# Global attention: maximum products in couples over four banks, score half steps over three

## What is computed

```python
h = NUM_HEADS                                   # 16 heads of 64
q = _split_heads(x @ Wq + bq, h)
k = _split_heads(x @ Wk + bk, h)
v = _split_heads(x @ Wv + bv, h)
pattern = jnp.einsum('bhid,bhjd->bhij', k, q) * scale
prob = jax.nn.softmax(pattern, axis=-2)         # over i, the k side
out = jnp.einsum('bhis,bhid->bhsd', prob, v)
concat = out.transpose(0, 2, 1, 3).reshape(b, s, h * dv)
return concat @ Wo + bo
```

## Time and profile before

| what | value |
|---|---|
| median of three runs | 5289.54 us (5285.4 to 5291.37) |
| profiled execution | 5297.28 us, span 5295.5 us |
| PE busy (share of the span) | 4716.1 us (89%) |
| DVE, ACT, POOL busy | 3549.8 (67%), 2216.3 (42%), 2746.9 us (52%) |
| mean granted clock of PE | 0.938 of 2.4 GHz |

### The profile page before, as it was taken

The page is one execution under the profiler, slowest core; times in us unless marked ns, Lnnn a source line. Parts: engine busy times, 40 slices in busy tenths (PEclk is TensorE's granted clock), DMA queues, the critical chain, the costliest instruction groups (busy, mean ns, idle before and its releaser), DMA issues.

```text
span 5295.5 us, 68189 instructions
## 1 busy us (share of the span) xinstructions
PE 4716.1 (89%) x21552; PEld 2860.2 (54%) x21552; DVE 3549.8 (67%) x4540; ACT 2216.3 (42%) x3456; POOL 2746.9 (52%) x1140
## 2 busy tenths in 40 slices
PE   5899999999998598788869999999999986987988
PEld 3455555555554375566634555555555534765756
DVE  4878878778775564454467787787788755634544
ACT  2344444444433254355323444443444333543553
POOL 0456566566567264265205665665665663632652
PEclk8999999999999798899979999999999997988989
DMA  1000000000000100000010000000000000000000
GB/s 40 5 5 1 5 5 1 5 5 1 5 2 1 52 1 33 17 1 10 24 36 5 5 1 5 5 1 5 5 1 5 2 29 24 1 33 17 1 33 17
DMA packets 78790, 59.22 MB, mean 11 GB/s; under 512 B 41304, under 2 KB 75392, under 8 KB 78464
## 3 DMA queue, kind: packets, MB, share of 16 engines
q1 hardware_dynamic: 78464, 54.93, 3.3%
HBM read 50.45 MB, written 4.19 MB: 10 GB/s over the span
## 4 chain that ended last, share of the span: by engine, by line
POOL 44%; issue 31%; PE 12%; DVE 7%; ACT 3%; POOLq 1%; DMA 1%; DVEq 0%; SPq 0%; ACTq 0%
POOL accp L610 34%; PE psum L1449 4%; POOL lp L632 4%; POOL accp L606 3%; PE psum L1324 2%; ACT lp L756 2%; POOL rnorm L622 1%; DVE lnr L391 1%; POOL qk_u L627 1%; PE psum L1462 1%; PE psum L361 1%; DVE qk_w L1009 1%; DVE lneg L1023 1%; PE psum L1370 1%; DVE ssq L997 1%
## 5 line engine op out<-in xcount | busy, mean ns | idle before, releaser
L610 POOL TENSOR_TENSOR accp<-accp,prob 128x1024 f32<-128x1024 f32 x640 | 1641.0, 2564 | 709.1 <-ACT prob L705 670.0
L705 ACT ACTIVATE prob<-psum 128x1024 f32<-128x1024 f32 x1024 | 1040.1, 1026 | 1694.6 <-PE psum L1227 1560.7
L896 DVE TENSOR_REDUCE mx<-psum 128x1 f32<-128x512 f32 x1920 | 1231.6, 683 | 408.3 <-PE psum L1204 370.1
L1238 PE MATMUL psum<-prob,vv 128*64 128x512 f32 x4096 | 994.9, 607 | 0.0
L1226 PE MATMUL psum<-qhh,klh 128*128 128x512 f32 x2048 | 844.4, 412 | 35.3 <-issue 14.6
L1227 PE MATMUL psum<-qlm,kh 65*128 65x512 f32 x2048 | 830.4, 405 | 0.0
L1204 PE MATMUL psum<-klh,qhh 128*128 128x512 f32 x1920 | 703.2, 425 | 50.4 <-DVE mx L896 47.8
L1204 PEld LDWEIGHTS psum<-klh,qhh 128*128 128x128 f32 x1920 | 341.9, 192 | 445.4 <-DVE mx L896 300.7
L1238 PEld LDWEIGHTS psum<-prob,vv 128*64 128x64 f32 x4096 | 249.6, 136 | 512.8 <-issue 372.3
L1226 PEld LDWEIGHTS psum<-qhh,klh 128*128 128x128 f32 x2048 | 399.8, 195 | 214.9 <-issue 92.7
L610 POOL TENSOR_TENSOR accp<-prob 128x1024 f32<-128x1024 f32 x64 | 153.8, 2403 | 680.9 <-ACT prob L705 675.9
(11 more groups left out here) (159 smaller groups left out, 6749.4 us busy)
## 6 DMA issues: line engine op xcount, KB each, us to landing
rot_l<-const_rot SPq DMA_DIRECT2D x6, 2048.0 KB, 8.0
wqkv_l<-L_ffn_wqkv SPq DMA_DIRECT2D x12, 768.0 KB, 9.5
w_l<-L_ffn_w SPq DMA_DIRECT2D x8, 682.0 KB
tok<-L_attn_x SPq DMA_DIRECT2D x32, 128.0 KB, 2.2
out<-tok SPq DMA_DIRECT2D x32, 128.0 KB, 1.7
wo_l<-L_ffn_wo SPq DMA_DIRECT2D x6, 512.0 KB, 10.0
w_l<-L_ffn_w SPq DMA_DIRECT2D x4, 640.0 KB
wqk<-L_attn_Wq SPq DMA_DIRECT2D x32, 64.0 KB, 2.1
```

Of the source, the lines that this page charges most:

```text
L610: pool.tensor_tensor(acc_p[cp][:], first[:], prob[kt % PRING][:], ALU.add).then_inc(pool_sum, 1)
L705: act.activation(prob[t % PRING][:], psum[:, S_BANK + 2 * (t % 2):S_BANK + 2 * (t % 2) + 2, :].rearrange("p a b -> p (a b)"), ACT.Exp, sca ...
L896: dve.tensor_reduce(mx4[:, j // CHUNKS, j % CHUNKS:j % CHUNKS + 1], ps, AX_X, ALU.max).then_inc(ring_free, 1)
L1238: mm = pe.matmul(psum[j * DH:(j + 1) * DH, O_BANK, :], vv[:, kt, s * DH:(s + 1) * DH], prob[t % PRING][:, j * T:(j + 1) * T], start=(kt == ...
```

## The change

The ring gets a fourth bank and the scores lose one. `RING = 4` with `M_BANK = 4`, `O_BANK = 3`, and `S_RING = 3` banks for the scores.

Maxima are made in couples: PE issues two matmuls into two neighbouring banks with one wait and one signal, and VectorE reduces both with one instruction (128x1024 to 128x2). A couple takes two places, and so do the turn and the sums, which keeps couples on even places. The thirds of a group are cut anew for couples.

Scores go by half steps: half j of step t uses bank (2t + j) mod 3 and waits for the exponential three halves back; each half has its own exponential of 512 columns (`s_full` and `exp_done` count halves). Whoever waits for a whole step waits for twice the count. The projection uses the same three banks from bank 1 on, so its fourth item waits until ScalarE and VectorE have read its first (`projected(G, 1)`), and the next head's first half waits for three items, the second for all four.

```diff
-RING = 3
-RING_MAX = KT * CHUNKS
-TURN_PLACES = (2, 1)
+RING = 4
+S_RING = 3
+MAX_TILES = KT * CHUNKS
+RING_MAX = MAX_TILES // 2
+PLACES = {"max": 2, "turn": 2, "sum": 2, "out": 1, "proj_v": 1}
...
-        S_BANK, O_BANK, M_BANK = 0, 4, 5
+        S_BANK, O_BANK, M_BANK = 0, 3, 4
...
-                cut0 = (n + 1) // 3
-                cut1 = cut0 + n // 3
+                cut0 = (n + 2) // 3
+                cut1 = cut0 + (n + 1) // 3
...
+        def project_bank(i):
+            return S_BANK + (i + 1) % S_RING
+
+        def score_bank(t, j):
+            return S_BANK + (2 * t + j) % S_RING
...
-                        act.wait_ge(s_full, G * STEPS + t + 1)
+                        act.wait_ge(s_full, 2 * (G * STEPS + t) + 1)
...
-                        act.activation(prob[t % PRING][:], psum[:, S_BANK + 2 * (t % 2):S_BANK + 2 * (t % 2) + 2, :].rearrange("p a b -> p (a b)"),
-                                       ACT.Exp, scale=float(ATT_SCALE)).then_inc(exp_done, 1)
+                        for j in range(2):
+                            if j:
+                                act.wait_ge(s_full, 2 * (G * STEPS + t) + 2)
+                            act.activation(prob[t % PRING][:, j * T:(j + 1) * T], psum[:, score_bank(t, j), :],
+                                           ACT.Exp, scale=float(ATT_SCALE)).then_inc(exp_done, 1)
...
-                def max_tile(rb, i, j):
-                    ps = ring_wait(rb, i)
-                    dve.tensor_reduce(mx4[:, j // CHUNKS, j % CHUNKS:j % CHUNKS + 1], ps, AX_X, ALU.max).then_inc(ring_free, 1)
+                def max_tiles(rb, i, j):
+                    dve.wait_ge(ring_full, OFF_RING + rb + i + PLACES["max"])
+                    qt, c = divmod(2 * j, CHUNKS)
+                    at = M_BANK + i % RING
+                    dve.tensor_reduce(mx4[:, qt, c:c + 2], psum[:, at:at + 2, :], AX_X, ALU.max).then_inc(ring_free, PLACES["max"])
...
+                    if i >= S_RING:
+                        projected(G, i - S_RING + 1)
                     for h in range(HALVES):
-                        mm = pe.matmul(psum[:, S_BANK + i, :], wqk_h[s][:, h, :], hT[:, h, i * T:(i + 1) * T],
+                        mm = pe.matmul(psum[:, project_bank(i), :], wqk_h[s][:, h, :], hT[:, h, i * T:(i + 1) * T],
...
+                def max_tiles(rb, r, s, j):
+
+                    qt, c = divmod(2 * j, CHUNKS)
+                    ring_slot(rb, r, PLACES["max"])
+                    for k in range(2):
+                        mm = pe.matmul(psum[:, M_BANK + r % RING + k, :], qhh[s][:, qt * P:(qt + 1) * P], klh[s][:, (c + k) * T:(c + k + 1) * T],
+                                       start=True, stop=True)
+                    mm.then_inc(ring_full, PLACES["max"])
...
-                    if t >= 2:
-                        pe.wait_ge(exp_done, G * STEPS + t - 1)
...
                     for j in range(2):
+                        if 2 * t + j >= S_RING:
+                            pe.wait_ge(exp_done, 2 * G * STEPS + 2 * t + j - S_RING + 1)
+                        elif projects and t == 0:
+                            projected(G + 1, QK_ITEMS - 1 + j)
                         cols = slice((2 * cp + j) * T, (2 * cp + j + 1) * T)
-                        ps = psum[:, S_BANK + 2 * (t % 2) + j, :]
+                        ps = psum[:, score_bank(t, j), :]
```

77 lines of the change are left out of this document (34 added, 43 removed).

## The result

The changed kernel takes **5328.2 us** (median of four runs, 5323.8 to 5338.0), the kernel before 5287.5 beside it: ratio 1.0082, 95% interval 1.0062 to 1.0101. It is slower by 0.8%, where 5299.5 with 5273 to 5320 was forecast: the sign of the sum was right, its size was not, and the time lies outside the range. The profiled execution took 5324.9 us (span 5322.8), 27.3 over the span before; the two medians are 41 apart.

What follows compares the result with a forecast made beforehand. PE was taken to set the pace of global attention, losing time only at few places. Terms for those places summed to +10 us on the 5289.5 us median: 5299.5 us, range 5273 to 5320.

Steps and rivals of the forecast that it cites:

- Output tiles split: Even heads' four output-tile groups: one tile between the steps and one behind costs 0.19 us per group, +10.9 us.
- Output tiles' wait: Even heads: a group's first output tile, behind two couples, waits for the first couple's reduction; 0.42 us per head, +5.9 us.
- Rival B: Head boundaries: VectorE's second normalisation product falls under GpSimd's add, delaying the first couple's reduction; 5307 to 5319 us, chance 0.14.
- Projection: The fourth item waits 0.32 us for its bank, uncovered ahead of even heads: +4.5 us, and +1.3 ahead of the loops.
- Odd entry: Entry to an odd head: PE's wait for the maxima shrinks from 2.64 to 2.0 us; 0.51 per head, -7.1 us.
- Even entry: Even heads: exponential waits shrink at ten jumps back, -1.9 us; second couple waits for a reduction at four others, +2.0.
- Inside heads: Pauses behind VectorE's adds in groups 7 and 13 of even heads go, less small three-bank waits: -5.6 us.
- Steady groups: Half steps do not make PE wait for exponentials in steady groups, with a margin of 0.40 us: 0.
- Clock: Slices at 1.2 GHz behind most entries to odd heads: the shorter wait wins only -2 us (-20 to +5).
- rival A: Entries to odd heads: shorter waits keep the clock up, and low clock goes; 5276 us, chance 0.16.
- C: Rival: small waits in groups 11 and 12 bring the clock down in every head; 90 us, 5390 us, chance 0.03.
- D: Rival: the output-tile split costs nothing and the entries win nothing; 5290 us, chance 0.12.

Runs made afterwards that it cites:

- run 9: The changed kernel with maxima made and reduced one by one, each with its own place, in the couples' order, output tiles still split: 5267.7 us, ratio 0.9927.
- run 10: The changed kernel, but VectorE reduces each couple by two instructions, each giving back its own place: 5292.0 us, ratio 0.9970.
- Run 7: The changed kernel, but GpSimd's add of step 6 in the first half waits for VectorE's add of step 5: 5323.2 us, ratio 1.0055.
- run 5: The changed kernel with 128 already met waits (64 instructions as built) in TensorE's stream ahead of the batch loop: 5326.0 us, ratio 1.0067.
- run 6: The changed kernel, but in the loop's heads the next pair's weight loads start only behind the eighth step's exponentials: 5328.9 us, ratio 1.0071.
- run 2: The changed kernel, but GpSimd's adds of steps 3, 6, 9 and 13 wait for VectorE's add just before: 5351.5 us, ratio 1.0117.
- run 4: The kernel before with only half-step scores and exponentials, on its four score banks, without couples or fourth ring bank: 5294.1 us, ratio 1.0012.

## Why the prediction failed, by its own steps

- **Output tiles split, +10.9.** Wrong in kind. Groups of 6.59 to 6.61 us with the tiles split (runs 9 and 10) against 6.59 with them together: 0. The new crossing, from an output tile to a score, takes 0.03 + 0.64 us in the starts, and the two intervals that it replaces took 0.43 + 0.23: the sum had 0.19 for it.
- **Output tiles' wait, +5.9.** This step failed. The place was right, the first tile behind two couples; so was the cause named, the add of step 5 queued ahead. But the add was taken at 2.1 us, and at 0.27 of wait. It became 3.26, the wait 1.3, and group 1 lost 0.43, groups 2 and 4 0.24 each: with group 5, which the sum did not have, 2.40 + 0.53 = 2.9 a head, 41 us where 5.9 stood. Run 7 parts this: with the add of step 5 back at 1.22, group 3 keeps 0.24 like its neighbours. So 1.25 a head came by the long add, and 0.24 in each of groups 2 to 4 by the one reduction, which gives both places back only at its end; run 10 removes both. What was missing is that the add's length is not a given: the row that I read (1859 ns) is a mean over 1.22 (steps 5 and 8 of even heads) and 1.5 to 2.1, set by who starts first, and the change moves both starts. With the add at 1.22, as in run 10, the wait is gone, tiles split and all.
- **Rival B** came true as an event and not as a price. In five of the ten heads behind a jump back VectorE's two products take 3.5 us (before 1.39 in all ten), the sign that the prediction named. But PE needs the first couple's places again only 0.7 to 1.3 us after even the late reduction has ended, and these five stretches (106.9 to 107.4) are no longer than the other five (107.1 to 107.9). The mechanism struck at the adds of steps 5 and 8 instead. The changed kernel's products at the jump shown above:

```profile
954.27 3.52 DVE L935 TENSOR_TENSOR oT<-o_raw,rcp 64x512 f32<-64x512 f32 x2
```

- **Projection, +4.5 and +1.3.** The fourth item comes 0.27 late in the starts and the pass behind it 0.07, in all 28 heads, where 0.32 stood. In odd heads the later wait for the last item covers it, as forecast (it ends 11.77 us behind the turn, before 11.93). Right.
- **Odd entry, -7.1.** The wait of 2.0 was met (2.0 by the starts). The stretch without low clock fell by 0.7 (91.34 to 90.6), of which 0.22 belongs to the inside of the head: 0.5 x 14 = 7. Right. (The steps to 657.65 add up to 657.71; the wait takes that up.)
- **Even entry.** The +2.0 did not come: the four entries without a jump took 26.2 us up to group 1's values for 26.5. The -1.9 was overrun by the code's second pause, +9 to +10 us, for which the sum had no term and which the one pause of before did not foretell: it depends on where the code lies.
- **Inside heads, -5.6.** Groups 6 to 14 gained 0.20 in even heads and 2 to 14 gained 0.22 in odd ones, 28 x 0.21 = 5.9. The size is right by luck: the sum had 0.35 in each even head and nothing in odd ones. **Steady groups, 0**: right, pairs of groups take 10.22 for 10.18.
- **Clock, -2.** In the profiled executions low clock in the 28 stretches fell from 85 to 38 us of slices at 1.2 GHz, worth some 20 us (14 slices of 1.54), and the loss covered it. That rival A's mechanism did this is not shown: run 5 has the changed kernel's odd entries and 65 us of such slices, run 6 has 41.
- **C** did not happen: the granted clock is 1.00 over 8 of the 14 odd stretches and 10 of the 14 even ones, though the three-bank ring's pauses of 0.06 and 0.10 stand in every head. **D** was right on the split, which costs nothing, and wrong on the entries.

In sum (profile): even heads +40.8, odd heads -19.1, outside +5.6 make +27.3. The parts' medians say of the even heads 34 in groups 1 to 4, 7 in group 5, 13 at the entry, 5 at the projection, less 3 in the rest: 56, of which less low clock gave 15 back. The medians differ by 13 us more than the profiles, because the profiled execution lay 9.8 above its kernel's median before and 3.3 below it after. The granted clock points to low clock (0.938 in that execution before, 0.940 to 0.943 in most others), but no trace shows it. The 5.6 outside sit in part where the loop over layers jumps back (a gap of 12.7 and 14.6 us for 10.8 and 11.7); what lengthens it was not tried.

## What to carry to other kernels

One instruction for two tiles saves the engine that runs it and delays the one that waits for the first tile. Where a ring of banks is the link, give each place back by itself, and read whether the saved engine was a bound at all. When two engines share a port, a mean duration in the profile can be two durations: look at them by place, and ask of each edit whether it moves a start past the other's. And a wait for an engine that is late but not full is removed by giving it less at that one place.

## What had not been expected of the hardware

- VectorE's add of 128x1024 took 1.22 us when it started up to 0.05 ahead of GpSimd's (in the kernel before 0.01 to 0.02 behind it by the records), 3.26 when it started 0.19 behind and 3.03 at 0.42 behind; GpSimd's took 3.4 to 3.5 in the first case and 2.37 in the others.
- A copy with one operand was stretched too: VectorE's 64x512 copy took 1.91 us when it started under a GpSimd add and 0.42 when it started ahead of one (run 2 and the changed kernel).
- Where in TensorE's code a loop starts was worth 9 us of 5320 in the profile: the same kernel with 64 idle instructions ahead of its loops has one pause of 1.5 us at a jump in the mean instead of one of 1.3 and one of 1.0. In run 4 it is one of 2.5 to 3.2 at five jumps of ten.
- Delaying 0.40 MB of loads away from the jump changed neither pause.
